# ScalarE's program as a loop over units, one table word per tile, and all sums of the next unit ahead of a unit's variances

## The reference, cut to what matters

```python
g = v.reshape(B_, G, C_ // G, H_, W_)              # _gn, G = 32
m = jnp.mean(g, axis=(2, 3, 4), keepdims=True)
s = jnp.var(g, axis=(2, 3, 4), keepdims=True)
return ((g - m) / jnp.sqrt(s + eps)).reshape(v.shape)
...
shifted = x[:, ch[:, None, None], iyc[:, :, None], ixc[:, None, :]]
shifted = shifted * mask[None]
kern = jnp.exp(-(kx * kx + ky * ky) / (2.0 * SIGMA * SIGMA))
kern = kern / kern.sum(axis=(1, 2), keepdims=True)
out = lax.conv_general_dilated(shifted, kern_c[:, None, :, :], ..., feature_group_count=C)
...
x = x + _L0_conv_ref(_gn(x), L0_conv_offset)
```

## Time and profile before

| | us |
|---|---|
| median of 3 runs | 1246.45 (1244.77 to 1249.37) |
| the profiled execution's own time | 1247.67 |
| its span in the profile | 1245.5 |
| busy: TensorE, VectorE, ScalarE, GpSimd | 860.3, 836.2, 649.8, 354.7 |
| moved by DMA | 403.30 MB, 324 GB/s on average |
| mean granted TensorE clock | 0.829 of full speed |

### The profile page before, as it was taken

One profiled execution on the slowest core, in us unless ns is written; L12 is line 12 of the kernel. 1 busy time (PEld: TensorE's weight loads), 2 busy tenths in 40 slices (PEclk: granted clock), 3 DMA queues, 4 the chain that ended last, 5 costly groups with the idle time before them and its releaser, 6 DMA issues.

```text
span 1245.5 us, 9666 instructions
## 1 busy us (share of the span) xinstructions
PE 860.3 (69%) x2176; PEld 417.6 (34%) x2176; DVE 836.2 (67%) x580; ACT 649.8 (52%) x514; POOL 354.7 (28%) x598
## 2 busy tenths in 40 slices
PE   2976775768676596657867768877968576886710
PEld 1433332334333243323433334333433332443310
DVE  5287496866848668584874957576776758557584
ACT  0464355544557644665455556544545565555561
POOL 5024232233321324312332321322233213222121
PEclk9997877978888797878978888887988788787855
DMA  9527969797997887889699997989998896998635
GB/s 383 226 106 294 384 227 407 285 386 314 337 403 298 325 349 274 363 289 399 236 374 372 348 401 283 401 343 381 372 352 332 326 411 250 401 349 310 283 135 245
DMA packets 46269, 403.30 MB, mean 324 GB/s; under 512 B 21648, under 2 KB 21648, under 8 KB 21648
## 3 DMA queue, kind: packets, MB, share of 16 engines
q0 software_dynamic: 30720, 201.40, 42.6%
q1 hardware_dynamic: 15504, 201.39, 39.9%
HBM read 201.38 MB, written 201.33 MB: 323 GB/s over the span
## 4 chain that ended last, share of the span: by engine, by line
DVE 26%; PE 20%; DMA 14%; ACT 12%; issue 10%; POOL 9%; ACTq 6%; DVEq 2%; POOLq 0%
PE sum_ps L273 16%; DMA xs<-x_dram 12%; ACT frame L344 6%; DVE smooth L519 6%; DVE smooth L516 6%; ACTq L329 5%; DVE xs L523 5%; DVE xs L526 5%; ACT unused L371 4%; DVE xs L529 3%; POOL small L233 3%; DMA out_dram<-xs 2%; POOL small L235 2%; DVEq L536 1%; POOL small L237 1%
## 5 line engine op out<-in xcount | busy, mean ns | idle before, releaser
L273 PE MATMUL sum_ps<-xs,bands 128*128 128x512 f32 x1024 | 511.9, 658 | 42.2 <-DVEq L425 22.1
L371 ACT ACTIVATE unused<-xs,small 128x4096 bf16<-128x4096 f32 x96 | 356.1, 3709 | 53.6 <-issue 51.3
L516 DVE SCALAR_TENSOR_TENSOR smooth<-frame,xs 128x1700 f32 (+5 forms) x96 | 163.5, 1703 | 308.7 <-ACT frame L351 217.2
L273 PE MATMUL sum_ps<-xs,halves 128*128 128x512 f32 x512 | 250.5, 646 | 98.5 <-DMA xs<-x_dram 98.4
L273 PEld LDWEIGHTS sum_ps<-xs,bands 128*128 128x128 f32 x1024 | 212.2, 213 | 292.6 <-issue 270.5
L344 ACT ACTIVATE frame<-xs,small (+1 forms) x96 | 222.8, 2321 | 63.6 <-DVE smooth L519 63.3
L523 DVE SCALAR_TENSOR_TENSOR xs<-smooth,small,xs 128x1700 f32 (+5 forms) x96 | 163.5, 1704 | 65.2 <-POOL small L245 62.9
L273 PEld LDWEIGHTS sum_ps<-xs,halves 128*128 128x128 f32 x512 | 104.8, 209 | 242.0 <-issue 242.0
L519 DVE SCALAR_TENSOR_TENSOR smooth<-frame,xs,smooth 128x1700 f32<-128x1700 f32 (+5 forms) x96 | 163.6, 1704 | 3.4
L526 DVE SCALAR_TENSOR_TENSOR xs<-smooth,small,xs 128x594 f32 (+9 forms) x96 | 159.8, 1664 | 3.4
L529 DVE SCALAR_TENSOR_TENSOR xs<-smooth,small,xs 128x594 f32 (+9 forms) x96 | 159.7, 1664 | 3.4
(11 more groups left out here) (85 smaller groups left out, 394.1 us busy)
## 6 DMA issues: line engine op xcount, KB each, us to landing
xs<-x_dram SPq DMA_DIRECT2D x96, 1024.0 KB, 11.1
xs<-x_dram POOLq DMA_DIRECT2D x192, 512.0 KB, 12.0
out_dram<-xs SPq DMA_DIRECT2D x96, 1024.0 KB, 8.8
out_dram<-xs POOLq DMA_DIRECT2D x192, 512.0 KB, 10.6
smooth<-offset_dram SPq DMA_DIRECT2D x1, 48.0 KB, 3.5
```

What stands on the lines that cost most here:

```text
L273: last = nc.tensor.matmul(sum_ps[u % 2][:, :], (FIRST, SAME, SECOND)[i], slot_px(n, c * BANK, (c + 1) * BANK), start=(i == 0 and c == 0), ...
L371: nc.scalar.activation(unused[:, :], slot_px(n), ACT.Square, bias=neg_mean[:, u % 2, i:i + 1], accum_out=squares[:, u % 2, i:i + 1]).then_ ...
L516: V.scalar_tensor_tensor(sm, frame_window(-1), side_w[:, bass.ds(n, 1), 0], frame_window(0), ALU.mult, ALU.add).wait_op(frame_ready, done_ ...
```

## The change

- TensorE: the three sums of unit u+1 stand ahead of the variances of u (`sums`), and the variances' matmuls are issued by tile, each behind its own wait on `squares_ready`. `sum_ps`, `mean_sum`, `neg_mean`, `squares` and `var` have one buffer in place of two; a copy `fill_mean` is made for the fills.
- ScalarE: a loop over units 1 to 30, with unit 0 and 31 written out. The order of its steps is as before, with one small copy more per unit. One table word per tile in place of four, taken apart by register arithmetic.
- VectorE: one loop over 96 tiles, one table word per tile in place of three, also taken apart in registers.
- GpSimd: its first 18 load DMAs stand behind the memsets and the `affine_select` that the selectors need, not ahead of them; the memsets of `slot_at` are gone.

TensorE, before, units 2 and 1: from the sum of tile (2, 1) on.

```diff
@@ gpsimd @@
-            for n in range(SLOTS):
-                load(n)
             V.memset(residues[:, :, :], 0.0).then_inc(pool_step, 1)
...
             V.affine_select(out=residues[:, :, :], in_=residues[:, :, :], compare_op=ALU.not_equal, fill=1.0, base=0,
                             pattern=[[-1, SET], [-SET, P // SET]], channel_multiplier=1).then_inc(pool_ready, 1)
+            for n in range(SLOTS):
+                load(n)
...
@@ tensor @@
+            def sums(u):
+                if u:
+                    pe.wait_ge(mean_sum_ready, u)
+                for i in range(UT):
+                    n = u * UT + i
+                    pe.wait_ge(loaded[n % SLOTS], 16 * (n // SLOTS + 1))
+                    pe.wait_ge(outer_loaded[n % SLOTS], 32 * (n // SLOTS + 1))
...
             def variances(u):
...
+                pe.wait_ge(squares_ready, UT * u + 1)
+                nc.tensor.matmul(var_ps[:, 0, 0:1], ALL, first, start=True, stop=False)
+                nc.tensor.matmul(var_ps[:, 1, 0:1], FIRST, first, start=True, stop=False)
+                pe.wait_ge(squares_ready, UT * u + 2)
...
             for u in range(UNITS):
                 if u + 1 < UNITS:
-                    sum_tile(u + 1, 0)
-                    sum_tile(u + 1, 1)
+                    sums(u + 1)
                 variances(u)
                 if u + 1 < UNITS:
-                    sum_tile(u + 1, 2)
                     means(u + 1)
@@ scalar @@
             def load_fill(n):
-                for register, word in ((kind_at, KIND), (from_at, FROM), (to_at, TO), (edge, EDGE)):
-                    act.reg_load(register, table[0:1, n, word:word + 1])
+                act.reg_load(entry, fills[0:1, bass.ds(n, 1)])
...
+            def means_to_fill(u):
+                nc.scalar.activation(fill_mean, neg_mean, ACT.Copy).then_inc(fill_mean_ready, 1)
+                act.wait_ge(fill_mean_ready, u + 1)
...
+            def unit_of(u, ahead=True):
+                fill_frame(u, 0)
+                next_fill(u, 0)
+                variances(u)
+                if ahead:
+                    sum_means(u + 1)
+                fill_frame(u, 1)
+                next_fill(u, 1)
+                if ahead:
+                    means(u + 1)
+                    square(u + 1, 0)
+                fill_frame(u, 2)
+                if ahead:
+                    next_fill(u, 2)
+                    means_to_fill(u + 1)
+                    square(u + 1, 1)
+                    square(u + 1, 2)
...
+            unit_of(0)
+            act.addr_align(256, max_nops=0)
+            with act.Fori(1, UNITS - 1) as u:
+                unit_of(u)
+            unit_of(UNITS - 1, ahead=False)
@@ vector @@
-            def tile_of(unit, i):
-                n = dve.snap(done_count, min_val=0, max_val=TILES - 1)
-                for register, word in ((kind_at, KIND), (to_pixel, DST), (from_pixel, SRC)):
-                    dve.reg_load(register, table[0:1, bass.ds(n, 1), word:word + 1])
+            def tile_of(n):
+                dve.reg_load(entry, windows[0:1, bass.ds(n, 1)])
...
+                kind_of = dve.snap(word >> FROM_BITS + TO_BITS)
+                base = dve.snap(slot, min_val=0, max_val=(SLOTS - 1) * PIX)
+                dve.reg_mov(to_pixel, base + ((word >> FROM_BITS) & (1 << TO_BITS) - 1))
...
+            with dve.Fori(0, TILES) as n:
+                tile_of(n)
```

More of the change, by code:

```diff
@@ L288, in variances @@
+                nc.tensor.matmul(mean_ps[:, 2:3], OF_SECOND, mean_sum, start=True, stop=True).then_inc(mean_ps_ready, 1)
             def variances(u):
-                first, middle, last = (squares[:, u % 2, i:i + 1] for i in range(UT))
-                pe.wait_ge(squares_ready, UT * (u + 1))
+                first, middle, last = (squares[:, i:i + 1] for i in range(UT))
                 if u >= 1:
                     pe.wait_ge(var_ready, u)
-                nc.tensor.matmul(var_ps[:, 0:1], ALL, first, start=True, stop=False)
@@ L305, in _ @@
+                nc.tensor.matmul(var_ps[:, 2, 0:1], OF_SECOND, middle, start=True, stop=False)
+                pe.wait_ge(squares_ready, UT * u + 3)
+                nc.tensor.matmul(var_ps[:, 1, 0:1], SECOND, last, start=False, stop=True)
+                nc.tensor.matmul(var_ps[:, 2, 0:1], ALL, last, start=False, stop=True).then_inc(var_ps_ready, 1)
+            sums(0)
             means(0)
@@ L341, in emit @@
                     b = target.with_bounds(min_val=PAD * PITCH, max_val=(PAD + H - rows) * PITCH)
-                    if n:
-                        act.wait_ge(smooth_ready, n)
+                    if not first:
+                        act.wait_ge(smooth_ready, done)
                     nc.scalar.activation(
@@ L379, in _ @@
+            act.reg_mov(slot, 0)
             load_fill(0)
@@ L381, in _ @@
             means(0)
+            means_to_fill(0)
             for i in range(UT):
-                square(0, i)
-            for u in range(UNITS):
-                ahead = u + 1 < UNITS
-                fill_frame(u * UT)
-                variances(u)
-                if ahead:
-                    sum_means(u + 1)
-                fill_frame(u * UT + 1)
-                if ahead:
-                    means(u + 1)
-                    square(u + 1, 0)
-                fill_frame(u * UT + 2)
-                if ahead:
-                    square(u + 1, 1)
-                    square(u + 1, 2)
+                square(0, i, first=(i == 0))
+            unit_of(0)
[3 more added lines that the diff above has]
+            unit_of(UNITS - 1, ahead=False)
         @block.vector
@@ L500, in _, with smooth_tile @@
             done_count = dve.alloc_register("done_count")
-            def smooth_tile(rows, cols, src, dst, n, done, unit, weights):
+            def smooth_tile(rows, cols, src, dst, n, done, weights):
                 around = frame[:, bass.ds(src - 1, rows * PITCH + 2)]
```

168 lines of the change are left out of this document (80 added, 88 removed).

## The result

| | us | beside the kernel before |
|---|---|---|
| median of 4 runs | 1335.67 (1330.98 to 1337.76) | 1247.58 (4 runs, 1244.77 to 1249.37) |
| ratio of the two | 1.0703 | 95% interval 1.0665 to 1.0741 |
| span of the profiled execution | 1335.4 | 1245.5 |
| mean granted TensorE clock | 0.815 | 0.829 |

The change makes the kernel 7% slower. The forecast was 1300, its range 1250 to 1345.

A forecast was written before the change was run, and what follows sets the result against it. The prediction took a loop of waits through a late load in a full DMA stretch as the bound. Span 1245.5 + 97 - 32 - 8 - 4 = 1298.5, then + 2.2 - 1.2, about 1300 us; range 1250 to 1345.

The forecast's parts named there:

- The bound: A loop of waits, not an engine; at unit 18, 36.4 us from an even unit's end to a late load's landing.
- The sums ahead of the variances: At pair boundaries, even units' variances wait for the sums of (u+1, 2): +97 us over 15 boundaries, 6.5 each.
- The closed path: Late rows of unit 18 delay its end, its slot's load and so unit 20; the boundary delays add to 97 us.
- What the same edit gives back: Frame gaps in even units go, odd units' weights up to 5 us sooner: -32 for 15 pairs, -8 for the last.
- the second case: Boundary sums at lower clock (20 us), odd units' stores and loads sooner in the full stretch (20): 1340, chance 0.15.
- Single buffers: One buffer in place of two costs nothing; without cover, a short wait per unit, less than 2.5 us.
- Table words at nothing: Fewer table loads and new register instructions on ScalarE and VectorE, costed together at nothing.
- The start: Memsets ahead of GpSimd's 18 load issues let first sums start sooner; unit 0's variances wait for tile 5: about 4 us gained.
- The last pair: The edit's gain in the last pair, -8 us, 5.9 of it the frame gap of unit 30.
- The third case: Load of (u+1, 2) lands less than 29 us after the even unit's end, nothing added: 1203, chance 0.14.
- The fourth: Longer pair lets DMA queues run empty, loads land 3 to 4 us sooner, delays and gains even: 1247, chance 0.09.
- The two rules: GpSimd contends with VectorE for SBUF (2.3 us taken at late variances); idle gaps throttle TensorE, some 20 us more in all.

The follow-up runs named there:

- e6: Changed kernel, and the same with TensorE's old order, each storing half of every tile: 1158.16 us in new order, 1117.58 us in old order.
- e2: Kernel before, with only the new order added (all three sums of u+1 ahead of the variances of u): 1327.66 us, ratio 1.066.
- e4: Changed kernel with the new order for even units only, the old order for odd ones: 1326.74 us, ratio 1.0652 to the kernel before.
- e1: Changed kernel with TensorE's old order (two sums of u+1, variances of u, third sum): 1213.8 us, ratio 0.9761 to the kernel before.
- e3: Changed kernel with the new order for odd units only, the old order for even ones: 1216.59 us, ratio 0.9764 to the kernel before.
- e9: Kernel before, with only the new start (GpSimd's first 18 load issues behind the memsets and the select): 1240.94 us, ratio 0.9946.
- e5: Changed kernel with TensorE's old order, plus three unused table loads per tile on ScalarE, absent from the program that ran: 1213.57 us.
- e11: Changed kernel with TensorE's old order, plus two unused table loads per tile on VectorE, absent from the program that ran: 1212.36 us.

## Why the prediction was right, and where it was off

**The bound.** Right for the changed kernel: a loop of waits through the landing of tile (e+3, 2). e6 shortened nothing but the transfers, and the pair followed them, by 11.7 us. With the old order the landing alone is not the bound: there the same cut took 5.9 us from a pair, and in the kernel before the rows began 6.2 us behind the landing on average.

**The sums ahead of the variances.** Right in place and mechanism (e2, e4). The term of +97 measured 15 x 7.0 = 105 between landing and rows, and at unit 18 the count of 9.1 + 4.6 met 13.7. The closed path held: the delays added up. (Redone from the trace before, the landings plus the sums plus 4.6 us give 93 us with sums of 7.1 us at ten boundaries and 9.1 at five, and 99 with the durations they took there; 97 lies between.)

**What the same edit gives back.** This is the step that was off. The gaps in even units went, as said, and even units became 1.7 us shorter, 26 in all. But the forecast also counted as gain that `weights` of the odd unit would come up to 5 us sooner. They came 0.6 us later on average (4.7 us after the end of the even unit for 4.1), and from that end to the issue of the load it stayed 15.6 us. So -32 was worth -26 at most. And it took the landing as fixed to the end of the even unit: it came 1.2 us later, with the load longer under way, +18. This was not the order's doing: with the order alone (e2) the landing comes 33.6 us after that end, as before, while it is 34.7 in e1, e3 and e4 and 34.8 in the changed kernel. It goes with the rest of the change, in whose kernels the odd units have less idle time. That their stores and loads so reach the full stretch sooner is what the second case had named; no run shows that this is the cause. With 105 for 97, -26 and +18 it is +98 for +65: 33 of the 36 us between forecast and result. The other half of the second case, sums at the lower clock, is seen in part: the last sums took 8.6 us on average, for 8.2 before and for the 7.1 that the forecast took at ten boundaries. That is 6 us in all beside the kernel before, and not 20.

The idle time tells the same, but was forecast too small: VectorE's wait for GpSimd grew by 202 us (62.9 before), not by about 100. I had left out that a frame that is no longer late adds its wait to this one: the waits for frames fell by 120.5, and much of this came inside the odd units and ahead of tile (e+2, 0), from where VectorE only reaches the next wait sooner.

**Single buffers.** No run isolates them; e1 has them and is faster than the kernel before, so any price is hidden in its gain.

**Table words at nothing.** In the time this held: e2 and the whole change cannot be told apart, though the +18 above came with this part of the edit and the start made up for half of it. With the new order a pair is the even unit, the way to the landing and 13 us, and the odd unit's own work is no term of it: its idle time fell from 94 us (e2) to 71, and the wait for `weights` took that up. As a statement on the edit the nothing was wrong: with the old order what is left beside the start is worth some 24 us. ScalarE is not in the path at the boundary of a pair, but VectorE waits for its frames inside the odd units. There I had read that odd units cost nothing, and did not ask what they could gain.

**The start.** 3.6 us for 4. Alone it gave 6.7 (e9): with the new order unit 0's variances wait for tile 5, as forecast.

**The last pair.** 4.1 us in place of 8; with this the sum is whole to within 1 us.

**The rivals.** The third case, faster, said that nothing is added once the landing comes less than 29 us after the end. That bound was wrong: the sums and the chain behind it take 13 us more, and in e6 the landing comes 23.3 us after the end and the order still costs 41 us. The fourth, cancelled, did not occur: loads took 1.2 us longer, not 3 to 4 less.

**The two rules.** The Trainium skill, GPSIMD Engine Reference, "Key points", on the shared SBUF interfaces: the trace agrees, since GpSimd's second step took 0.19 us at 811.14 beside an idle VectorE and 2.76 beside a row instruction. The Trainium skill, TensorE: Matmul & The Clock Gate, "HAM oscillation", asks to do the matmuls together ahead of a wait for DMA. Here the grouped matmuls wait for loads that come one by one. The granted clock in the stretch up to the landing was 0.72, for 0.90 before, and the grouped order was the slowest of the three.

## What to carry to other kernels

Before moving work ahead of a short step, ask what the step releases and how late the moved work's input is: an in-order engine makes everything behind a wait as late as the wait. The engine that waits longest isn't the one to relieve: 231 of the 257 us of ScalarE's wait for sums went here, and the kernel became 7% slower; what counted was 13 us per pair in which VectorE stood and the DMA engines fell to a third of their share. A change of several parts should be tried part by part, since this one holds a gain of 2.4% (e1, with its repeats the fastest full kernel here) under its loss.

## What the runs showed of the hardware

- A table load into a register takes 0.27 to 0.30 us at its fastest, but up to 1.78 on ScalarE and 1.66 on VectorE (the rows of e5 and e11 above). With one load in place of four, and other register work with it, ScalarE's wait ahead of the copy of the means fell from 2.5 to 0.5 us a time (78.3 and 14.3 us in 31 waits), where three loads at their fastest are 0.8 us.
- A load's time on the way went with the bytes that the kernel moves: GpSimd's part took 19.2 us from issue to landing in the changed kernel and 12.5 with a quarter of all bytes gone, so a third of the time for a quarter of the bytes.
- Eight matmuls of 512 columns took 7.11 us at a granted clock of 1.00 (all at 2.4 GHz) behind the landing in e1, and 9.14 in the changed kernel, in a stretch with 0.85 (part of it at 1.2 GHz), for the same work. Ahead of it the clock was 0.72, in a stretch in which TensorE waited 7.00 and 5.26 us for loads; in e1 it was 0.84. The stretches of e1, with the columns of the windows above:

```profile
691.00:723.84 32.84, 20.32 (x57) 9.62 (x55) 19.41 (x16) 18.28 (x17) 7.46 (x14) 0.84 1.01 404
723.84:734.54 10.70, 9.79 (x27) 4.69 (x28) 5.87 (x3) 3.14 (x4) 5.40 (x13) 1.00 0.95 374
```

- A register load whose value is never read was not in the program that ran (96 loads each in e5 and e11): an experiment that adds cost has to use what it adds, and its trace must be counted.
